# Gated cross-attention with a routed expert layer on one core: routing work reordered across engines in the first pairs of tiles, the loops over slots written out, the passage between the stages rearranged, and a small matmul put ahead of the scores

## The chip, the cores and the metric

The kernel runs on one core of one Trainium2 chip. The metric is the device time of one execution in microseconds (us). Of the kernel before, three runs gave 657.65, 660.46 and 661.85 us, so its median is 660.46 us. One more execution was profiled; it took 661.32 us, of which 659.5 us lie between its first and its last instruction.

## The reference, cut to what matters

```python
# x, ctx: (16, 256, 256); wq, wk, wv: (256, 256); Wg: (8, 256); W1, W2: (8, 704, 256); W3: (8, 256, 704)
def attention(q, c, wq, wk, wv):          # queries from c, keys and values from q
    Q, K, V = c @ wq, q @ wk, q @ wv
    return softmax(Q @ K.T, axis=2) @ V

def experts(x, Wg, W1, W2, W3):           # 4096 tokens
    scores = x @ Wg.T
    topk_scores, topk_idx = top_k(scores, 2)
    y = einsum('teh,edh->ted', silu(x @ W1) * (x @ W2), W3)
    return sum over the two chosen experts of topk_scores * y

x = x + tanh(g_xattn[0]) * attention(ctx, layernorm(x), wq, wk, wv)
x = x + tanh(g_ffn[0]) * experts(layernorm(x), Wg, W1, W2, W3)
```

## The kernel before

The work has two stages on the same five engines. Engine programs are written out by hand, one per engine, and are tied together by semaphores; nothing reorders them. An engine that waits holds up everything behind it in its own program.

**First stage, steps n = 0 to 15, one batch of 256 rows each.** TensorE multiplies the context with the weights (`z`, `v`), forms the scores, sums, turns the probabilities and multiplies them with the values. ScalarE copies results out of PSUM, takes the exponents, and squares the weights of half an expert per step (`squares`, lines 682 to 693). `weight_sum` (line 865) adds these squares over the partitions on TensorE, VectorE makes the power of two out of them by which that half expert is scaled (`scales`, line 1041), and ScalarE (`w_hi`, line 715) and VectorE (`lo12`, `lo3`, lines 1061 to 1074) split the scaled weights into two float16 parts. VectorE also adds the residual, takes the second moments of the new rows and routes ten of the sixteen batches already here: `AT_STEP` (line 71) says at which step batch m is routed. To route a batch takes a chain over four engines: `second_moments` (VectorE), the power -1/2 (GpSimd, `deviations` or `second_deviations`), `high_rows` (VectorE) and `norm_rows` (ScalarE) for the two parts of the normed rows, `low_rows` (GpSimd), `turn_rows` and `router` (TensorE, ScalarE copying between them by `copy_rows`), `choose` (VectorE, the two best experts), `rank` (TensorE, the place within the expert), `slots` (VectorE) and `scatter` (GpSimd, four indirect DMAs that write the rows into a buffer in HBM sorted by expert).

**Second stage, slots i = 0 to 38.** Slots 0 to 31 are pairs of tiles of 128 rows of one expert, 32 to 38 single tiles. SP fetches the rows of slot i+2, TensorE turns them (`turn_gathered`), ScalarE copies them, TensorE multiplies with W1 (`to_hidden`, 36 matmuls), ScalarE applies silu (`gate`), TensorE multiplies with W2 (30 matmuls), VectorE multiplies the two (`mixed` for the piece of 64 partitions, `combined` for the rest), ScalarE and VectorE split the result (`high`, `low`), TensorE multiplies with W3 (`to_output`, 17 matmuls for each tile), ScalarE scales it (`copy_product`) and GpSimd adds it to the rows in HBM (`add_rows`, an indirect DMA that adds). Each such add waits until the one before it has landed. The last six batches are routed during the pairs 0 to 5 (`AT_PAIR`, line 72), so that batch 10+i goes through the chain above in pair i. When all are placed, VectorE works out the list of slots 8 to 38 (`other_slots`, lines 1251 to 1283) and releases it by `s_map`; before that SP cannot fetch slot 8.

`over_slots` (line 401) lets each engine run its step for slots -2 to 7 written out, 8 to 23 as two passes of a loop with eight steps in it, and the rest written out again. GpSimd has a loop of its own for the slots 8 to 31 (line 633).

The rows of rsqrt in the pairs are made by these lines, in this order (lines 626 to 632 of GpSimd's program):

```python
for i in range(EARLY):
    if i + 1 in AT_PAIR:
        second_deviations(AT_PAIR[i + 1])
        low_rows(AT_PAIR[i + 1])
    if i in AT_PAIR:
        scatter(AT_PAIR[i])
    add_rows(i, i % 4)
```

Of the kernel before, what the change touches and what calls it, by code (L numbers as in the profile page):

```python
# [7 lines left out]
ALU = mybir.AluOpType  # L8
# [8 lines left out]
P = 128  # L17
# [6 lines left out]
def gated_cross_attention_and_experts(nc, x, ctxT, g_xattn, g_ffn, wqT, wkT, wv, WgT, W1T, W2T, W3T, out):  # L24
# [70 lines left out]
    with ExitStack() as ctx:  # L95
# [253 lines left out]
        def pair(i):  # L349

            return not isinstance(i, int) or i < PAIRS
# [13 lines left out]
        def at_least(eng, s, v):  # L365

            if not (isinstance(v, int) and v <= 0):
                eng.wait_ge(s, v)

        def wait_alone(eng, s, v):  # L370


            if not isinstance(v, int):
                v = eng.to_reg(v)
                eng.wait_ge(s_const, CONSTS)
                eng.wait_ge(s, v)
            elif v > 0:
                eng.wait_ge(s, v)
# [22 lines left out]
        def over_slots(eng, step, take=lambda i, n: None, planned=lambda: None):  # L401


            def written(a, b):
                for i in range(a, b):
                    step(i, i // 2, i % 4, i % UNROLL, lambda m: 0 <= m < SLOTS)
# [16 lines left out]
        def _(sp):  # L423
# [59 lines left out]
            for k in range(2):  # L483
                sp.wait_ge(s_scat[k], 16 * KT * TOP_K * ((COUNTED + 1 - k) // 2))
                sp.wait_ge(s_x2st[k], 16 * (5 - k))
            sp.wait_ge(s_xn2, 9)
# [18 lines left out]
            def moe_step(i, j, k4, u, on):  # L505
                k = k4 % 2
                if isinstance(i, int) and i == EARLY - 2:
                    pads()
                    all_rows()
                if on(i + 2):  # L510

                    wait_alone(sp, s_id, i + 1)
# [8 lines left out]
        def _(pool):  # L521
# [85 lines left out]
            scatter(IN_STEPS - 1)  # L607
            low_rows(IN_STEPS)
# [5 lines left out]
            def add_rows(i, k4):  # L614

                for t, half, t8 in tiles(i, k4):
                    if t8 % 2 == 0:
                        if not (isinstance(t, int) and t == 0):
                            pool.wait_ge(s_add[1], 16 * half)
                    else:  # L620
                        pool.wait_ge(s_add[0], 16 * half + 16)
                    wait_alone(pool, s_y_copied, t + 1)
                    pool.indirect_dma_start(  # L623
                        out=out[:, :], out_offset=bass.IndirectOffsetOnAxis(ap=id_s[:, t8:t8 + 1], axis=0),
                        in_=y_s[:, t8 % 4, :], in_offset=None, compute_op=ALU.add).then_inc(s_add[t8 % 2], 16)
# [12 lines left out]

        @block.scalar
        def _(act):  # L640
# [40 lines left out]

            def squares(u):
# [10 lines left out]
                ins.then_inc(s_sq, 1)  # L693

# [740 lines left out]
```

## Time and profile before

| what | us |
|---|---|
| median of three runs | 660.46 |
| lowest, highest | 657.65, 661.85 |
| the profiled execution | 661.32 |
| its span, first to last instruction | 659.5 |
| TensorE busy with matmuls | 589.5 (89%) |
| VectorE, ScalarE, GpSimd busy | 318.4, 329.6, 269.1 |
| mean granted clock of TensorE | 0.962 of full speed |

In the page and the answers PE is TensorE, PEld its weight loads, DVE VectorE, ACT ScalarE, POOL GpSimd and SPq, ACTq, POOLq the DMA queues. A granted clock of 1.00 is TensorE's 2.4 GHz, 0.50 would be 1.2 GHz. Matmuls overlap in the records, so the time of a group is best taken from its start to the start of the next. A bracket behind a row says how long the engine was idle before it, and who ended that. Idle time of an engine costs time only where that engine's work is what the end waits for; here TensorE has most of it, so the gaps in its row are what is to be explained.

### The profile page before, as it was taken

How to read it: one execution, taken by the hardware profiler on the slowest of the kernel's cores; microseconds unless marked ns; L12 is line 12 of the kernel's file. 1: busy time of each engine (PE TensorE's matmuls, PEld its weight loads, DVE VectorE, ACT ScalarE, POOL GpSimd, SP SyncE). 2: the span in 40 equal slices, each digit the busy share in tenths (PEclk: the TensorE clock that was granted, in tenths of full speed). 3: DMA queues.
4: the chain of work that ended last, by engine and by line, in shares of the span. 5: the costliest groups of instructions: out<-in, count | busy, mean ns of one | idle time of the engine just before them, and what ended most of it. 6: DMA issues, size and time to landing. Idle time of an engine off the chain costs nothing.

```text
span 659.5 us, 15092 instructions
## 1 busy us (share of the span) xinstructions
PE 589.5 (89%) x4765; PEld 511.8 (78%) x4766; DVE 318.4 (48%) x860; ACT 329.6 (50%) x474; POOL 269.1 (41%) x245
## 2 busy tenths in 40 slices
PE   5898989898688967789699999799999999999995
PEld 4787878777567855678598989698989898988783
DVE  2488877797656434456333333243433343343332
ACT  3778787887734243433344444244444444444442
POOL 3155565655513655546133333223233333333322
PEclk9899999999878987899799999899999999999999
DMA  8476666855412322215232323132323232322322
GB/s 254 142 233 188 219 203 220 258 169 165 149 35 85 68 60 68 59 34 138 58 59 43 58 36 52 31 54 43 59 43 59 42 56 39 52 42 43 50 43 25
DMA packets 52372, 61.53 MB, mean 93 GB/s; under 512 B 7632, under 2 KB 46160, under 8 KB 52304
## 3 DMA queue, kind: packets, MB, share of 16 engines
q1 hardware_dynamic: 34656, 38.15, 19.2%
q0 software_dynamic: 13296, 18.23, 16.0%
q10 hardware_dynamic: 4352, 4.20, 1.8%
q8 instruction: 48, 0.79, 0.5%
q14 instruction: 20, 0.16, 0.1%
HBM read 36.90 MB, written 23.66 MB: 92 GB/s over the span
## 4 chain that ended last, share of the span: by engine, by line
PE 61%; DVE 12%; ACT 10%; issue 8%; POOL 5%; DMA 2%; another core or an unknown queue 1%; SPq 0%; POOLq 0%; ACTq 0%; DVEq 0%
PE psum L923 30%; PE psum L963 18%; PE psum L818 4%; PE psum L932 4%; PE psum L943 2%; DMA w_in<-in_W3T 2%; ACT w_hi L715 2%; POOL rows_by_expert L586 2%; DVE w_lo L1072 2%; ACT arena L678 2%; ACT w_hi L687 1%; ACT w_hi L691 1%; DVE w_lo L1065 1%; POOL out L623 1%; PE psum L856 1%
## 5 line engine op out<-in xcount | busy, mean ns | idle before, releaser
L623 POOL DMA_INDIRECT out<-w_in,id_s x71 | 126.8, 1786 | 249.2 <-ACT w_in L767 132.4
L923 PE MATMUL psum<-arena,w_hi 128*128 128x256 f16 x1408 | 217.3, 278 | 5.5 <-issue 4.1
L923 PEld LDWEIGHTS psum<-arena,w_hi 128*128 x1408 | 140.3, 100 | 24.7 <-issue 6.2
L923 PE MATMUL psum<-arena,w_lo 128*128 128x256 f16 x704 | 136.9, 277 | 0.0
L749 ACT ACTIVATE arena<-psum 128x1024 f16<-128x1024 f16 (+1 forms) x39 | 36.9, 947 | 95.3 <-PE psum L943 94.8
L818 PE MATMUL psum<-arena 128*128 128x256 f32 x256 | 66.3, 404 | 19.0 <-ACT arena L701 19.0
L1353 DVE SCALAR_TENSOR_TENSOR arena<-psum,h_unit,arena 128x1280 f32<-128x1280 f32 x32 | 49.6, 1550 | 63.8 <-PE psum L923 63.8
L586 POOL DMA_INDIRECT rows_by_expert<-xn2r,slot_i x64 | 66.3, 1036 | 33.8 <-issue 17.4
L923 PEld LDWEIGHTS psum<-arena,w_lo 128*128 x704 | 70.2, 100 | 9.3
L818 PEld LDWEIGHTS psum<-arena 128*128 128x128 f32 x256 | 47.9, 197 | 28.0 <-ACT arena L701 22.4
L1347 DVE SCALAR_TENSOR_TENSOR arena<-psum,h_unit,arena 64x256 f32<-64x256 f32 x32 | 15.7, 491 | 92.3 <-ACT arena L740 92.2
L738 ACT ACTIVATE arena<-psum,w_unscale 64x256 f32<-64x256 f32 x32 | 15.0, 468 | 89.4 <-PE psum L923 89.3
L963 PE MATMUL psum<-w_hi,arena 128*128 x396 | 57.7, 281 | 2.2 <-DVE arena L1370 2.2
L963 PE MATMUL psum<-w_hi,w_in 128*128 x385 | 55.5, 280 | 0.0
L767 ACT ACTIVATE w_in<-psum,wsum 128x256 f32<-128x256 f32 x71 | 33.2, 467 | 43.8 <-PE psum L963 21.9
L963 PEld LDWEIGHTS psum<-w_hi,arena 128*128 128x128 f16 x396 | 38.9, 101 | 7.7 <-issue 2.4
L740 ACT ACTIVATE arena<-psum,w_unscale 128x1280 f32<-128x1280 f32 x32 | 42.5, 1328 | 0.4
L963 PEld LDWEIGHTS psum<-w_hi,w_in 128*128 128x128 f16 x385 | 37.6, 100 | 5.1
L715 ACT ACTIVATE w_hi<-w_in,w_scale 128x1408 f16<-128x1408 f32 x16 | 23.5, 1468 | 24.6 <-DVE w_scale L1047 18.2
L963 PE MATMUL psum<-w_lo,arena 128*128 x216 | 31.5, 284 | 0.0
L818 PE MATMUL psum<-arena,qk 128*128 128x256 f32 x128 | 30.6, 382 | 0.0
L943 PE MATMUL psum<-ident,xa 128*128 128x128 f16 x284 | 22.6, 221 | 8.7 <-DMA xa<-rows_by_expert 5.9
(183 smaller groups left out, 906.4 us busy)
## 6 DMA issues: line engine op xcount, KB each, us to landing
xa<-rows_by_expert SPq DMA_DIRECT2D x71, 136.0 KB
w_in<-in_W1T SPq DMA_DIRECT2D x8, 704.0 KB
w_in<-in_W3T SPq DMA_DIRECT2D x8, 640.0 KB
w_in<-in_W2T SPq DMA_DIRECT2D x8, 640.0 KB
arena<-in_ctxT SPq DMA_DIRECT2D x16, 256.0 KB
xa<-in_x SPq DMA_DIRECT2D x16, 256.0 KB, 6.0
out<-xa ACTq DMA_DIRECT2D x16, 256.0 KB
out<-w_in,id_s POOLq DMA_INDIRECT x71, 4.4
```

The source lines that it names most:

```text
L586: pool.indirect_dma_start(out=xs[:, :], out_offset=bass.IndirectOffsetOnAxis(ap=slot_i[:, k, col:col + 1], axis=0), in_=xn2r[:, m % ROWS, ...
L623: pool.indirect_dma_start(out=out[:, :], out_offset=bass.IndirectOffsetOnAxis(ap=id_s[:, t8:t8 + 1], axis=0), in_=y_s[:, t8 % 4, :], in_of ...
L715: act.activation(w12[0][:, :, n * H:(n + 1) * H], w12_in[:, k], ACT.Copy, scale=w_scale[:, 0:1].bitcast(F32)).then_inc(s_hi12, 1)
L740: act.activation(act_g[:, 0:KF * N2], g_ps, ACT.Silu, scale=w_unscale[:, 0, bass.ds(expert[u], 1)].bitcast(F32)).then_inc(s_silu, 1)
L749: act.activation(xg_t[:, k, :, :, 0:n], xt_ps[:, :, :, 0:n], ACT.Copy).then_inc(s_xgt, 1)
L767: act.activation(y_s[:, t8 % 4, :], y_ps[t8 % 2], ACT.Copy, scale=wsum[:, t8:t8 + 1]).then_inc(s_y_copied, 1)
L818: ins = pe.matmul(dst[:, t, :], left[:, c, t * P:(t + 1) * P], right[:, c, :], start=(c == 0), stop=(c == 1))
L923: ins = pe.matmul(flat_ps[:, j * N2:(j + 1) * N2], w12[w_part][:, c, bass.ds(e * (2 * H) + j * P, P)], xg_t[:, k, x_part, c, :], start=(q ...
L932: ins = pe.matmul(dst, xg_t[:, k, x_part, c, 0:P], w12[w_part][:, c, bass.ds(e * (2 * H) + at, n)], start=(q == 0 and c == 0), stop=(q == ...
L943: ins = pe.transpose(xt_ps[:, h, c, half * P:(half + 1) * P], xg[:, k, half, at:at + P // 2].bitcast(F16), ident16[:])
L963: ins = pe.matmul(y_ps[t8 % 2], hid_p[k4 % 2][:, c * n + h * P:c * n + (h + 1) * P], w3[w_part][:, r, bass.ds(e * D, D)], start=(q == 0), ...
L1353: dve.scalar_tensor_tensor(out=hid[:, 0:KF * N2], in0=u_ps, scalar=h_unit[:, 0, bass.ds(e, 1)].bitcast(F32), in1=act_g[:, 0:KF * N2], op0= ...
```

## The change

It computes the same. On each engine it changes where work stands in the program:

- **The sum of squares in front of the scores.** `weight_sum(n)` moves on TensorE from behind `router` and `rank` to ahead of the scores of step n. It gets waits of its own: for `s_rcopy` (that `choose` of the batch routed in step n-1 is through) and for `s_place`, because its result lies in the PSUM bank of the router. `router` and what follows wait for `s_half` of the same step. On VectorE `scales` moves ahead of `slots`.
- **The passage.** Slot 0 is turned and copied within step 15 (ahead of `values(14)` and of ScalarE's `w_hi` of step 15). SP fetches slot 0 a wait earlier. TensorE begins slot 0 when `s_lo12` is 15, and waits for 16 only before the sixth chunk; `turn_probs(15)` moves behind the first four chunks. ScalarE's last `w_hi` of W3, the table of silu and the wait for `s_unit` go behind step 15. `units` moves forward on VectorE, `choose(9)` ahead of `lo3(7)`.
- **The pairs with routing.** GpSimd works out the power of batch 10+i+1 in pair i, behind `low_rows` of batch 10+i, and the two adds of a pair are set apart, one at each end of its turn. GpSimd's wait for the stores of all batches (`s_x2st`) now stands ahead of `scatter(9)` and `low_rows(10)`. VectorE has `high_rows` at the front of the step and `second_moments` ahead of `combined`; ScalarE has `norm_rows` ahead of the copies; TensorE has `rank` behind the second half of the output of slot i-2.
- **Slots written out.** The loops go; all 39 slots are written out on every engine.

The core of the diff:

```diff
 # over_slots
-            written(-2, 0)
-            take(0, EARLY)
-            written(0, EARLY)
-            planned()
-            with eng.Fori(0, 2) as r:
-                take(UNROLL * r + EARLY, UNROLL)
-                for u in range(UNROLL):
-                    step(UNROLL * r + EARLY + u, UNROLL // 2 * r + (EARLY + u) // 2, u % 4, u, lambda m: True)
-            take(PAIRS - UNROLL, UNROLL)
-            written(PAIRS - UNROLL, PAIRS)
-            take(PAIRS, SINGLES)
-            written(PAIRS, SLOTS + 1)
+            for i in range(-2, SLOTS + 1):
+                if i >= 0 and i % UNROLL == 0:
+                    if i == EARLY:
+                        eng.wait_ge(s_map, 2)
+                    take(i, min(UNROLL, SLOTS - i))
+                step(i, i // 2, i % 4, i % UNROLL, lambda m: 0 <= m < SLOTS)
 # GpSimd
             second_deviations(IN_STEPS)
-            scatter(IN_STEPS - 1)
-            low_rows(IN_STEPS)
 
             for k in range(2):
                 pool.wait_ge(s_x2st[k], 16 * (B // 2))
             pool.wait_ge(s_dummy, 16)
...
-            for i in range(EARLY):
-                if i + 1 in AT_PAIR:
+            for i in range(SLOTS + 1):
+                if i >= 2 and pair(i - 2):
+                    add_rows(i - 2, 1)
+                if i == 0:
+                    scatter(IN_STEPS - 1)
+                if i - 1 in AT_PAIR:
+                    scatter(AT_PAIR[i - 1])
+                if i in AT_PAIR:
+                    low_rows(AT_PAIR[i])
+                if i + 1 in AT_PAIR and i >= 0:
                     second_deviations(AT_PAIR[i + 1])
-                    low_rows(AT_PAIR[i + 1])
-                if i in AT_PAIR:
-                    scatter(AT_PAIR[i])
-                add_rows(i, i % 4)
-            with pool.Fori(EARLY // 4, PAIRS // 4) as q:
-                for k4 in range(4):
-                    add_rows(4 * q + k4, k4)
-            for i in range(PAIRS, SLOTS):
-                add_rows(i, i % 4)
+                if i >= 1:
+                    add_rows(i - 1, 0)
 # TensorE, first stage
             def weight_sum(u):
 
                 pe.wait_ge(s_sq, u + 1)
                 at_least(pe, s_half, u)
+                if u - 1 in AT_STEP:
+                    pe.wait_ge(s_rcopy, AT_STEP[u - 1] + 1)
+                if u - 2 in AT_STEP:
+                    pe.wait_ge(s_place, AT_STEP[u - 2] + 1)
...
                 if live(n):
+                    weight_sum(n)
                     pe.wait_ge(s_z_copied, n + 1)
                     pe.wait_ge(s_t1_copied, n + 1)
                     product(sc_ps, x_t, z_s).then_inc(s_sc, 1)
                 if n in AT_STEP:
                     router(AT_STEP[n])
+                if live(n):
+                    pe.wait_ge(s_half, n + 1)
+                if n - 1 in AT_STEP:
+                    rank(AT_STEP[n - 1])
                 if n == COUNT_STEP:
                     count(COUNTED)
-                if n - 1 in AT_STEP:
-                    rank(AT_STEP[n - 1])
-                if live(n):
-                    weight_sum(n)
+                if n == B - 1:
+                    pe.wait_ge(s_t1_copied, B)
+                    turn_gathered(0, 0, 0)
                 if live(n - 1):
                     values(n - 1)
...
-            pe.wait_ge(s_lo12, 2 * E)
             pe.wait_ge(s_map, 1)
 # VectorE, pairs
                 if chosen:
                     choose(AT_PAIR[at - 1])
+                if at in AT_PAIR:
+                    high_rows(AT_PAIR[at])
                 if on(i):
                     if pair(i):
                         mixed(i, expert[u])
                     weights_and_rows(i, j, k4, expert[u])
                     if at == 0:
                         residual(B - 1)
+                        slots(IN_STEPS - 1)
...
-                    if at in AT_PAIR:
-                        high_rows(AT_PAIR[at])
+                    if at + 1 in AT_PAIR:
+                        second_moments(AT_PAIR[at + 1])
                     combined(i, expert[u])
-                    if at == 0:
-                        slots(IN_STEPS - 1)
                     low(i, k)
```

GpSimd's program in one of the pairs with routing, from the first add of a pair on. In the kernel before both adds stand together, the power of the next batch comes behind them, and the rows of that batch directly behind the power:

```order
L623 DMA out<-w_in,id_s 4224x256 [waits s_y_copied,s_add1]
L623 DMA out<-w_in,id_s 4224x256 [waits s_y_copied,s_add0]
L574 TENSOR_SCALAR var_eps<-mv 128x2 [waits s_rcopy,s_mv2]
L576 TENSOR_TENSOR rstd<-var_eps,neg_half 128x2 [waits s_ve]
L595 COPY xn2r<-token 128x2 [waits s_xh,s_xf]
L596 TENSOR_TENSOR xn2r<-arena,xn2r 128x2x256
L586 DMA rows_by_expert<-xn2r,slot_i 33792x272 [waits s_xn2,s_slot]
L586 DMA rows_by_expert<-xn2r,slot_i 33792x272 x3
```

In the changed kernel, at the same place:

```order
L603 DMA out<-w_in,id_s 4224x256 [waits s_y_copied,s_add1]
L603 DMA out<-w_in,id_s 4224x256 [waits s_y_copied,s_add0]
L569 DMA rows_by_expert<-xn2r,slot_i 33792x272 [waits s_xn2,s_slot]
L569 DMA rows_by_expert<-xn2r,slot_i 33792x272 x3
L578 COPY xn2r<-token 128x2 [waits s_xh,s_xf]
L579 TENSOR_TENSOR xn2r<-arena,xn2r 128x2x256
L557 TENSOR_SCALAR var_eps<-mv 128x2 [waits s_rcopy,s_mv2]
L559 TENSOR_TENSOR rstd<-var_eps,neg_half 128x2 [waits s_ve]
```

The power (L574, L576; now L557, L559) moved behind `low_rows`, and belongs to the batch after the one whose rows are made there; the first add is that of the pair before. The program is a cycle, so that the two adds still stand side by side.

TensorE's program in a step of the first stage in which one batch goes through the router and the one before it is ranked, before:

```order
L818 MATMUL psum<-arena 128x256 [waits s_t1_copied,s_z_copied]
L818 MATMUL psum<-arena 128x256 x3
L856 MATMUL psum<-wg_c,arena 128x8 [waits s_half,s_place,s_wg,s_rcopy,s_t2_copied]
L856 MATMUL psum<-wg_c,arena 128x8 x3
L831 MATMUL psum<-mask,before 128x16 [waits s_seen1,s_rcopy]
L832 MATMUL psum<-seen,ones 128x16
L870 MATMUL psum<-ssq,ones_f 128x1 [waits s_half,s_sq]
```

and in the changed kernel:

```order
L872 MATMUL psum<-ssq,ones_f 128x1 [waits s_rcopy,s_half,s_sq]
L803 MATMUL psum<-arena 128x256 [waits s_t1_copied,s_z_copied]
L803 MATMUL psum<-arena 128x256 x3
L841 MATMUL psum<-wg_c,arena 128x8 [waits s_half,s_place,s_wg,s_rcopy,s_t2_copied]
L841 MATMUL psum<-wg_c,arena 128x8 x3
L816 MATMUL psum<-mask,before 128x16 [waits s_seen1,s_rcopy,s_half]
L817 MATMUL psum<-seen,ones 128x16
```

The sum of squares moved to the front and now waits for `s_rcopy`; the scores are queued behind it.

## Rows read from the trace of the kernel before

**Rows 1.** The page, its first line.

```profile
span 659.5 us, 15092 instructions
```

**Rows 2.** Busy time of engines by stretch; a row: stretch, length, engines, PEclk, DMA, GB/s.

```profile
17.40:184.47 167.07, 143.31 (x783) 123.56 (x781) 127.34 (x433) 133.62 (x228) 90.99 (x97) 0.97 0.60 192
184.47:198.73 14.26, 13.19 (x97) 10.86 (x98) 6.39 (x26) 4.58 (x6) 0.41 (x1) 0.84 0.08 24
198.73:286.93 88.20, 70.74 (x595) 59.79 (x595) 39.05 (x139) 31.11 (x43) 46.50 (x48) 0.88 0.27 66
286.93:322.53 35.60, 26.77 (x222) 22.29 (x221) 21.79 (x65) 12.63 (x15) 17.49 (x14) 0.86 0.37 95
322.53:413.60 91.07, 91.07 (x866) 81.76 (x863) 33.40 (x47) 40.03 (x48) 29.81 (x16) 1.00 0.29 49
413.60:424.00 10.40, 6.30 (x43) 5.02 (x44) 1.91 (x2) 1.66 (x3) 2.26 (x1) 0.84 0.13 18
```

**Rows 3.** Waits between 18 and 180 us: waited for, us, times, longest.

```profile
PE psum L818 <- ACT arena L701: 19.0, 14, 2.8
ACT w_hi L715 <- DVE w_scale L1047: 18.2, 11, 3.2
```

**Rows 4.** Timeline of PE, scores of step 12: start, us, what, [idle before].

```profile
138.84 1.99 PE L818 MATMUL psum<-arena 128*128 128x256 f32 x8 [1.17 <-ACT arena L701]
```

**Rows 5.** Timeline of DVE, steps 11 and 12.

```profile
132.10 1.65 DVE L1134 TENSOR_TENSOR nbias<-nmax,rstd 128x2 f32<-128x2 f32 x1
...
140.23 0.35 DVE L1183 SCALAR_TENSOR_TENSOR xn2r<-psum,rstd,mask 128x8 f32<-128x8 f32 x2
...
143.71 0.44 DVE L1134 TENSOR_TENSOR nbias<-nmax,rstd 128x2 f32<-128x2 f32 x1
```

**Rows 6.** Timeline of PE, the passage from step 15 to slot 0.

```profile
171.58 3.42 PE L818 MATMUL psum<-arena 128*128 128x256 f32 x8 [2.76 <-ACT arena L701]
...
180.92 0.61 PE L943 MATMUL psum<-ident,xa 128*128 128x128 f16 x8 [2.77 <-DVE w_lo L1065]
...
184.47 1.03 PE L923 MATMUL psum<-arena,w_hi 128*128 128x256 f16 x4 [1.40 <-ACT arena L749]
```

**Rows 7.** Timeline of POOL, one pair with routing.

```profile
260.34 1.61 POOL L623 DMA_INDIRECT out<-w_in,id_s  x1 [0.30 <-issue]
264.45 1.59 POOL L623 DMA_INDIRECT out<-w_in,id_s  x1 [2.50 <-DMA out<-w_in,id_s]
...
266.39 0.73 POOL L576 TENSOR_TENSOR rstd<-var_eps,neg_half 128x2 f32<-128x2 f32 x1
271.98 0.96 POOL L595 COPY xn2r<-token 128x2 int32<-128x2 int32 x1 [4.87 <-ACT arena L659]
...
274.22 1.07 POOL L586 DMA_INDIRECT rows_by_expert<-xn2r,slot_i  x1 [0.17 <-issue]
...
279.42 1.62 POOL L623 DMA_INDIRECT out<-w_in,id_s  x1 [0.30 <-issue]
```

**Rows 8.** Waits of the whole execution.

```profile
DVE shift L1104 <- POOL rstd L576: 35.7, 4, 9.4
...
PE psum L831 <- DVE xn2r L1183: 19.8, 6, 5.4
```

**Rows 9.** Timeline of PE, pairs 4 to 8 and 16.

```profile
263.61 0.60 PE L811 MATMUL psum<-ident,xa 128*128 128x128 f32 x4
...
266.35 0.96 PE L856 MATMUL psum<-wg_c,arena 128*128 128x8 f32 x8
...
293.93 0.18 PE L831 MATMUL psum<-mask,before 128*128 128x16 bf16 x1 [2.90 <-DVE xn2r L1183]
...
318.42 1.01 PE L943 MATMUL psum<-ident,xa 128*128 128x128 f16 x8 [5.93 <-DMA xa<-rows_by_expert]
...
417.70 1.02 PE L923 MATMUL psum<-arena,w_hi 128*128 128x256 f16 x4 [4.10 <-issue]
```

**Rows 10.** Timeline of DVE, first instruction of the list of slots.

```profile
306.14 0.15 DVE L1253 SCALAR_TENSOR_TENSOR begin<-done,region_of 1x8 f32<-1x8 f32 x1
```

More of the change, by code:

```diff
@@ L349, in pair @@
         def pair(i):
-            return not isinstance(i, int) or i < PAIRS
+            return i < PAIRS
         def tiles(i, k4):
@@ L365, in at_least @@
         def at_least(eng, s, v):
[L367 to L377, printed above, removed]
+            if v > 0:
                 eng.wait_ge(s, v)
@@ L506, in moe_step @@
                 k = k4 % 2
-                if isinstance(i, int) and i == EARLY - 2:
+                if i == -1:
+                    sp.wait_ge(s_xn2, 9)
+                    sp.wait_ge(s_x2st[0], 16 * 5)
+                if i == EARLY - 2:
                     pads()
@@ L763, in copy_product @@
                 act.wait_ge(s_wsum, i + 1)
-                if not (isinstance(t, int) and t < 4):
+                if t >= 4:
                     act.wait_ge(s_add[t8 % 2], 16 * (half - 1))
@@ L778, in moe_step @@
                 if at in AT_PAIR:
+                    norm_rows(AT_PAIR[at])
                     copy_rows(AT_PAIR[at], x10_ps)
-                if on(i + 1):
+                if i >= 0 and on(i + 1):
                     copy_turned(i + 1, 1 - k)
@@ L863, in count, with turn_gathered @@
                 pe.matmul(cnt_ps, ones[:], seen[:, m % 2, 0, :], start=True, stop=True).then_inc(s_cnt, 1)
+            def turn_gathered(i, j, k):
+                pe.wait_ge(s_row[k], landed(i, j))
+                for half in range(2 if pair(i) else 1):
+                    for h in range(2):
+                        for c in range(KD):
+                            at = h * (D // 2) + c * (P // 2)
+                            ins = pe.transpose(xt_ps[:, h, c, half * P:(half + 1) * P],
+                                               xg[:, k, half, at:at + P // 2].bitcast(F16), ident16[:])
+                ins.then_inc(s_xt, 1)
             def weight_sum(u):
@@ L934, in to_hidden_rows @@
                 return ins
-            def turn_gathered(i, j, k):
-                pe.wait_ge(s_row[k], landed(i, j))
-                for half in range(2 if pair(i) else 1):
-                    for h in range(2):
-                        for c in range(KD):
-                            at = h * (D // 2) + c * (P // 2)
-                            ins = pe.transpose(xt_ps[:, h, c, half * P:(half + 1) * P],
-                                               xg[:, k, half, at:at + P // 2].bitcast(F16), ident16[:])
-                ins.then_inc(s_xt, 1)
             def turn_hidden(i):
@@ L999, in moe_step @@
                         to_hidden_rows(g1_ps[:, 1, :], HB - HL, HB, expert[u], k).then_inc(s_g, 1)
-                    if at is not None and at - 1 in AT_PAIR:
-                        rank(AT_PAIR[at - 1])
-                        if AT_PAIR[at - 1] == B - 1:
-                            count(B)
                 if on(i - 2) and pair(i - 2):
                     to_output(i - 2, (k4 - 2) % 4, 1, expert[u - 2])
+                if at == 0:
+                    rank(IN_STEPS - 1)
+                if at - 1 in AT_PAIR and at > 0:
+                    rank(AT_PAIR[at - 1])
+                    if AT_PAIR[at - 1] == B - 1:
+                        count(B)
                 if on(i):
@@ L1332, in weights_and_rows @@
                 dve.wait_ge(s_row[k], landed(i, j))
-                if not (isinstance(i, int) and i < 4):
+                if i >= 4:
                     dve.wait_ge(s_y_copied, ts[-1][0] - 7)
@@ L1336, in weights_and_rows @@
                                   ALU.mult).then_inc(s_wsum, 1)
-                if not (isinstance(i, int) and i < 4):
+                if i >= 4:
                     for t, half, t8 in ts:
```

100 lines of the change are left out of this document (49 added, 51 removed).

## The prediction

> **What bounds the kernel now.** I read the busy time by stretch first [rows 2]. The steady pairs show what the kernel can do: pairs 8 to 15 take 91.07 us, all of it TensorE's at full clock, so a pair is 11.4 us and nothing but fewer matmuls shortens it. The stretches to be won are those where TensorE has gaps. The first stage lasts 167 us, 24 of them without a matmul. Slot 0 takes 14.3 us. The five pairs 1 to 5 take 88.2 us, pairs 6 and 7 35.6 us, and around pair 16 there is a hole. I call S the start of the scores of step 15 (171.58 [rows 6]), G1 the start of pair 1 (198.73), G6 that of pair 6 (286.93), G8 that of pair 8 (322.53) [rows 2].
>
> Then I read the waits. In the first stage TensorE waits 19.0 us for the copy of z, and ScalarE 18.2 us for the scale of the weights [rows 3]. In the pairs VectorE's `high_rows` waits up to 9.4 us for GpSimd's power, and TensorE's `rank` 19.8 us over six times for `choose` [rows 8]. GpSimd's timeline says why [rows 7]: first add at 260.34, the second 4.1 us later because it waits for the first to land, then the power, then 4.87 us without work until ScalarE has made the normed rows that wait for this very power (`high_rows`, `combined`, `high` and `norm_rows` stand between), then four scatters, and the next first add at 279.42. That ring is 19.1 us long, and pairs 2 to 5 run at its pace, not at TensorE's.
>
> **The change part by part.** The sum is made against the profiled execution: a span of 659.5 us [rows 1] and 1.8 us around it, 661.3, which is 0.9 over the median.
>
> *Pairs 1 to 5.* A pair with routing needs 11.4 us of TensorE and two small groups, at most 0.60 + 0.96 us by their rows, some 1.3 as they overlap with what follows [rows 2, 9]: 12.7 us. With the power a pair ahead the ring is cut: `high_rows` finds its power made, and ScalarE makes the rows while GpSimd scatters. What stays is GpSimd's own work in a row: 4.1 from the first add to the second, 1.9 for that one, 5.2 for the scatters, 2.2 for copy and `low_rows`, 1.0 for the power, together 14.4 us [rows 7]; where the copy takes 0.2 instead of 0.96, 13.6. This is 1 to 1.7 us a pair more than TensorE needs. The lag gathers over four pairs to 4 to 7 us. I take it that most of it is absorbed: a power needed for `high_rows` may come late by about 2 us before `combined` is late, and `combined` and `choose` have about 2.5 more before TensorE needs them. I charge 1 us.
>
> Pair 1 has a wait of its own. GpSimd may now scatter batch 9 only when the stores of batches 14 and 15 have landed, and ScalarE issues these behind `high(0)`, about 2 us after G1. With 3.5 us to land (an estimate; the trace shows no row for it; bounds 2 and 6), 4.9 for the scatters, 1.3 and 1.0, the power of batch 11 comes at G1 + 13, and behind it `high_rows`, `mixed` and `slots` at G1 + 15, which the router of batch 11 waits for. So pair 1 takes 15.9 instead of 12.7. The gap of 3 us on TensorE is followed by slow matmuls, as everywhere here: pairs 1 to 5 run at a mean clock of 0.88 [rows 2]. I charge 1.6. Sum: 5 x 12.7 + 3.2 + 1.6 + 1.0 = 69.3 against 88.2, a gain of 18.9 (bounds: 25 with no wait at all; 13 if GpSimd sets all five pairs at 14.4 and the stores land late).
>
> *The passage, S to G1.* Today 27.2 us. TensorE waits 2.77 us for `lo12` before it turns slot 0 and 1.40 for ScalarE, which does the last W3 and loads the silu table first [rows 6]. Both go, since slot 0 is turned and copied within step 15. The first chunks run at half clock now, 1.03 us for four matmuls [rows 6] against 0.60 later; the stretch from 184.47 has a mean clock of 0.84, which is 2.3 us of work lost [rows 2]. The scores at S are slow as well, 3.42 us against 1.99 [rows 4, 6]. I count 4.2 of waits, 2.3 and 1.4 of clock: 7.9. What is late next is `values(15)`, because ScalarE does W3 and the table (about 3 us) ahead of the copy of the probabilities; six chunks of slot 0 cover that. Bounds 3 (a new wait there, the clock stays low) and 10.
>
> *Pairs 6 and 7.* The wait of 2.90 us for `rank` [rows 9] goes as low work of pair 5 is earlier, with 1.6 of slow clock behind it. The list of slots stays: it starts at 306.14 [rows 10], and 12.3 us later TensorE turns slot 8 [rows 9]. It hangs on `low(6)`, which stays in its place, so TensorE's wait of 5.9 stays too. Gain 4.5 (bounds 2 and 6).
>
> *The loops.* At the start of pair 16, where the second pass begins, TensorE waits 4.10 us for nothing that the trace shows [rows 9]. It is the only pair boundary in the stage with such a wait, and the only one at which a taken branch lies. The stretch of 10.40 us holds 6.30 of matmuls, at 0.84 [rows 2]: 4.1 and 1.8 of clock, 5.9 us gained. Bounds: 0, if filling the instructions of a written-out pair costs as much once, and 6.
> The Trainium skill, "Runtime: NRT & Kernel Launch", section "Instruction fetch mechanics", says that prefetch is purely sequential and that a taken branch to a target outside the window stops the engine for a fetch. The trace agrees, with the 4.10 us.
>
> *The first stage.* ScalarE's 18.2 us of waiting for the scale go, but the exponents behind `w_hi` need the scores and VectorE's maxima, which don't come sooner in a step where a batch is ranked. There the change costs: the scores are queued behind `weight_sum`, which now waits for `choose`. In step 12 `choose` writes its last piece at 140.23 + 0.35, the scores started at 138.84 [rows 4, 5]: 1.9 us later. There are nine such steps among 3 to 15. In the other steps the maxima come 0.3 us earlier and `w_hi` 1 us, and the step shortens by 1 to 1.8 us. Adding up a cycle of three steps on TensorE, VectorE and ScalarE I get 30.8 where the trace has 31.3. Steps 0 and 1, with nothing routed, give 2. In all 3.5 us gained (bounds 8 gained, 5 lost).
> One row speaks of a clash: VectorE's `nbias` takes 1.65 us at 132.10 and 0.44 at 143.71 [rows 5]; the first lies over GpSimd's `low_rows`. It is there before as after, so I count nothing.
> The Trainium skill, "SBUF — State Buffer", section "Who interferes with whom", says that a VectorE instruction with two SBUF inputs contends with a GpSimd instruction that reads SBUF, and that the second fully blocks. The 1.65 us agree. By it the sum would lose up to 1.5 us wherever the moved `scales` and maxima fall on `low_rows` anew, 7.5 for five steps; by the row, none.
>
> Sum: 18.9 + 7.9 + 4.5 + 5.9 + 3.5 = 40.7; 661.3 - 40.7 = 620.6, against the median 660.46 some 619.7.
>
> **The rivals.**
> 1. *The scores behind `choose` lengthen the first stage.* For it: 1.9 us in nine steps [rows 4, 5], and VectorE, busy 127 of 167 us [rows 2], can't simply be earlier. Against it: in the step after, ScalarE gains back what it waited [rows 3]. If nothing is gained back: 9 x 1.9 = 17 lost instead of 3.5 gained, 640.
> 2. *The pairs stay at GpSimd's old pace.* If another wait takes the place of the power (the landing of an add, the stores), pairs 1 to 5 stay near 88: 619.7 + 18.9 = 639. Against it: GpSimd's work in a row is 14.4, and its idle 4.87 is caused by the power alone [rows 7].
> 3. *Slower: written-out slots stall TensorE on its instructions.* The 16 pairs of the loop are now fetched as straight code. Each stall like that at pair 16 costs 5.9 [rows 2, 9]; six of them eat the other gains (34.8), and from eight on the kernel is slower by over 1%; one in each of 16 would give 625.6 + 94 = 720. Against it: pairs 0 to 7 and 24 to 31 are straight code today and show no such gap.
> 4. *1 and 2 together*, about 659: no change that can be told.
>
> **How the numbers follow.** Chances: forecast 0.76, with a range of its own from 608 to 633 (the bounds of the parts, which are 13 to 25, 3 to 10, 2 to 6, 0 to 6 and -5 to 8, added as independent deviations give about -11 and +13); rival 1 0.10; rival 2 0.07; both 0.03; rival 3 0.02; 0.02 for more gain than the range. The range takes in rivals 1 and 2: 608 to 640. One per cent (6.6 us) is about what a measurement of this kernel can tell from no change. Faster by over 1%: 0.76 + 0.10 + 0.07 + 0.02 = 0.95; same 0.03; slower 0.02.
>
> **What would show it.** Pairs 2 to 5: starts of `to_hidden` 12.7 to 14.4 us apart; GpSimd without the 4.9 us gap before its copy; no wait of `high_rows` over 3 us but in pair 1. Pair 1: near 16 us, ended by `slots`. Passage: S to G1 near 19 us. Slot 8: still a wait of about 6 us for the rows. Pair 16: no gap. First stage: scores start right behind `choose` in ranked steps, and S lies at 168. I am wrong if S is later than 172, if pairs 2 to 5 are over 16 us apart, or if gaps "issue" turn up in pairs 8 to 23.

## The result and the profile after

The changed kernel takes 626.7 us (median of 4 runs, 626.39 to 627.07) against 660.87 us (657.65 to 661.85) before, measured side by side: a ratio of 0.950, 95% interval 0.947 to 0.953. The profiled execution has a span of 625.0 us, 34.5 less than before [rows 1]. By the marks of the prediction:

| stretch | before, us | after, us | gained | forecast |
|---|---|---|---|---|
| start to S | 171.58 | 173.64 | -2.1 | 3.5 |
| S to G1 | 27.15 | 18.45 | 8.7 | 7.9 |
| G1 to G6 | 88.20 | 69.42 | 18.8 | 18.9 |
| G6 to G8 | 35.60 | 31.66 | 3.9 | 4.5 |
| G8 to the end | 336.97 | 331.83 | 5.1 | 5.9 |

The busy time by stretch, columns as in [rows 2], which it answers:

```profile
17.40:173.64 156.24, 140.13 (x747) 121.46 (x745) 115.04 (x407) 125.55 (x215) 88.98 (x89) 0.96 0.63 198
173.64:192.09 18.45, 16.86 (x136) 14.52 (x136) 14.90 (x54) 13.43 (x21) 6.32 (x8) 1.00 0.24 76
192.09:208.06 15.97, 11.83 (x105) 10.26 (x106) 6.63 (x28) 5.50 (x7) 7.04 (x9) 0.97 0.21 70
208.06:261.51 53.45, 53.45 (x489) 47.56 (x490) 33.90 (x109) 26.62 (x37) 36.96 (x40) 0.95 0.36 84
261.51:293.17 31.66, 24.38 (x222) 21.23 (x222) 20.94 (x62) 10.86 (x13) 18.62 (x15) 0.89 0.46 115
384.24:570.00 185.76, 185.76 (x1762) 166.71 (x1761) 70.16 (x100) 83.41 (x100) 61.99 (x33) 1.00 0.28 47
```

Pairs 2 to 5 (208.06 to 261.51) are now TensorE's without a gap, 12.66 us each in three of the four. The written-out slots at 384.24 to 570.00 have no gap either: the hole of [rows 9] at pair 16 is gone. What is left is a gap in pair 1, one in pair 7, and a first stage that became longer. The gain of 18.8 us from G1 to G6 isn't spread evenly: before, pairs 1 to 5 took 15.05, 13.98, 19.66, 19.74 and 19.77 us (starts of `to_hidden`), now they take 15.97, 15.47 and three times 12.66. So pairs 3 to 5 give 21.2 us, and pairs 1 and 2 are 2.4 us slower.

The waits of the first stage on TensorE (waited for, us, times, longest; to be read beside the 19.0 us of [rows 3], which are gone):

```profile
PE psum L872 <- DVE xn2r L1179: 9.4, 6, 2.3
PE psum L841 <- DVE halves L1041: 4.4, 2, 3.0
PE psum L872 <- ACT w_hi L676: 1.2, 1, 1.2
```

L872 is `weight_sum` (the sum of squares), L1179 the last piece of `choose`, L841 the router, L1041 the shift that makes the scale (`scales`, which signals `s_half`). The second row is a wait that the prediction doesn't have: the router of a step waits for that step's scale, since both are in PSUM bank 7. The timeline of TensorE in step 14 shows what it drags along:

```profile
157.69 1.99 PE L803 MATMUL psum<-arena 128*128 128x256 f32 x8
162.71 1.84 PE L841 MATMUL psum<-wg_c,arena 128*128 128x8 f32 x8 [3.03 <-DVE halves L1041]
164.41 3.76 PE L803 MATMUL psum<-arena 128*128 128x256 f32 x8
...
173.64 1.97 PE L803 MATMUL psum<-arena 128*128 128x256 f32 x8
```

After a gap of 3.03 us the values take 3.76 us, where the scores at S, with no such gap ahead, take 1.97. The stretch behind this gap, and the first 5.4 us of pair 2, behind the gap that ends pair 1, have a granted clock of 0.50, which is the level of 1.2 GHz (busy time by stretch, columns as above):

```profile
162.71:168.00 5.29, 5.29 (x17) 4.46 (x18) 0.77 (x3) 2.61 (x6) 4.29 (x6) 0.50 0.87 314
208.06:213.50 5.44, 5.44 (x27) 3.88 (x28) 3.81 (x10) 1.85 (x2) 4.52 (x6) 0.50 0.47 153
```

This one step is where the first stage loses. The scores of step 14 start at 157.69, against 159.22 before; from there to S it takes 15.95 us, against 12.36. In step 14 VectorE makes the scale only behind `high_rows`, and `high_rows` waits for GpSimd's power (timeline of VectorE):

```profile
161.58 0.16 DVE L1100 SCALAR_TENSOR_TENSOR shift<-mv,rstd 128x2 f32<-128x2 f32 x1 [0.95 <-POOL rstd L550]
162.32 0.14 DVE L1041 TENSOR_SCALAR halves<-psum 128x1 int32<-128x1 int32 x1
```

The busy time of the first stage up to S in the kernel before, to be read beside the first row of the busy time after:

```profile
17.40:171.58 154.18, 135.16 (x742) 117.15 (x740) 120.25 (x410) 124.46 (x214) 84.25 (x89) 0.99 0.62 199
```

TensorE is without a matmul for 16.1 us now and was for 19.0 us before. Its gaps became shorter, by 2.9 us; what makes S later are 5.0 us more of matmul time, at a mean clock of 0.96 instead of 0.99. The 5.29 us at half clock in step 14 are 2.6 of these 5.0.

Pair 1, on GpSimd, VectorE and TensorE (timelines):

```profile
197.29 1.03 POOL L569 DMA_INDIRECT rows_by_expert<-xn2r,slot_i  x1 [13.09 <-DMA out<-xa]
...
204.55 0.16 DVE L1100 SCALAR_TENSOR_TENSOR shift<-mv,rstd 128x2 f32<-128x2 f32 x1 [7.73 <-POOL rstd L559]
...
206.67 1.54 PE L841 MATMUL psum<-wg_c,arena 128*128 128x8 f32 x8 [3.58 <-DVE place L1112]
```

The scatters of batch 9 start when the stores have landed, G1 + 5.2 (forecast 5.5). That the two numbers are close is luck: ScalarE issues the last stores at 191.90 to 192.80, at G1 and not 2 us behind it, and they land 4.5 to 5.4 us later, not 3.5. `high_rows` starts at G1 + 12.5, the router of batch 11 at G1 + 14.6 (forecast 13 and 15). GpSimd in the pairs after, which answers [rows 7]:

```profile
240.36 1.17 POOL L579 TENSOR_TENSOR xn2r<-arena,xn2r 128x512 f16<-128x512 f32 x1
241.61 0.19 POOL L557 TENSOR_SCALAR var_eps<-mv 128x2 f32<-128x2 f32 x1
241.89 0.73 POOL L559 TENSOR_TENSOR rstd<-var_eps,neg_half 128x2 f32<-128x2 f32 x1
243.24 1.75 POOL L603 DMA_INDIRECT out<-w_in,id_s  x1 [0.62 <-ACT w_in L751]
247.52 1.56 POOL L603 DMA_INDIRECT out<-w_in,id_s  x1 [2.53 <-DMA out<-w_in,id_s]
249.39 1.00 POOL L569 DMA_INDIRECT rows_by_expert<-xn2r,slot_i  x1 [0.30 <-issue]
```

The idle 4.87 us ahead of its copy is gone; the next first add is at 256.95, a ring of 13.7 us instead of 19.1.

### The profile page after: what moved, and what is told of

The parts are those of the page before. It is cut to its first block, busy times and chain, and to the rows that moved or that the text cites. A ratio compares the mean times of both kernels' runs of the same rounds, so it can differ in the third digit from the quotient of the medians.

```text
span 625.0 us, 14783 instructions
## 1 busy us (share of the span) xinstructions
PE 581.5 (93%) x4765; PEld 510.1 (82%) x4765; DVE 315.8 (51%) x859; ACT 329.6 (53%) x473; POOL 271.7 (43%) x245
## 4 chain that ended last, share of the span: by engine, by line
PE 78%; DVE 10%; ACT 4%; issue 3%; POOL 2%; DMA 1%; POOLq 0%; SPq 0%; DVEq 0%; ACTq 0%
PE psum L928 34%; PE psum L957 20%; PE psum L803 12%; PE psum L937 4%; PE psum L857 2%; PE psum L841 2%; PE psum L796 2%; DVE w_lo L1068 1%; DVE w_lo L1061 1%; PE psum L946 1%; ACT w_hi L664 1%; DVE xa L1139 1%; DMA out<-xa 1%; DVE stats L1147 1%; ACT arena L659 1%
## 5 line engine op out<-in xcount | busy, mean ns | idle before, releaser
L928 PE MATMUL psum<-arena,w_hi 128*128 128x256 f16 x1408 | 213.4, 275 | 0.5 <-DVE xa L1139 0.4
L928 PEld LDWEIGHTS psum<-arena,w_hi 128*128 x1408 | 138.0, 99 | 17.8 <-issue 1.0
L928 PE MATMUL psum<-arena,w_lo 128*128 128x256 f16 x704 | 135.4, 274 | 0.0
L569 POOL DMA_INDIRECT rows_by_expert<-xn2r,slot_i x64 | 68.4, 1069 | 34.0 <-issue 17.7
L957 PE MATMUL psum<-w_hi,w_in 128*128 x385 | 53.5, 273 | 0.0
L751 ACT ACTIVATE w_in<-psum,wsum 128x256 f32<-128x256 f32 x71 | 33.2, 467 | 18.8 <-PE psum L957 18.8
L803 PE MATMUL psum<-wv_s,arena 128*128 128x256 f32 x128 | 30.2, 379 | 0.0
```

The lines of the kernel that those rows point to most:

```text
L569: pool.indirect_dma_start(out=xs[:, :], out_offset=bass.IndirectOffsetOnAxis(ap=slot_i[:, k, col:col + 1], axis=0), in_=xn2r[:, m % ROWS, ...
L751: act.activation(y_s[:, t8 % 4, :], y_ps[t8 % 2], ACT.Copy, scale=wsum[:, t8:t8 + 1]).then_inc(s_y_copied, 1)
L803: ins = pe.matmul(dst[:, t, :], left[:, c, t * P:(t + 1) * P], right[:, c, :], start=(c == 0), stop=(c == 1))
L928: ins = pe.matmul(flat_ps[:, j * N2:(j + 1) * N2], w12[w_part][:, c, bass.ds(e * (2 * H) + j * P, P)], xg_t[:, k, x_part, c, :], start=(q ...
L957: ins = pe.matmul(y_ps[t8 % 2], hid_p[k4 % 2][:, c * n + h * P:c * n + (h + 1) * P], w3[w_part][:, r, bass.ds(e * D, D)], start=(q == 0), ...
```

## The experiments

Marks of all kernels, us, each from one profiled execution; the ratio is to the kernel before on the same chip, with its 95% interval:

| kernel | S | S to G1 | G1 to G6 | G6 to G8 | from G8 | ratio |
|---|---|---|---|---|---|---|
| before | 171.58 | 27.15 | 88.20 | 35.60 | 336.97 | 1 |
| after | 173.64 | 18.45 | 69.42 | 31.66 | 331.83 | 0.950 (0.947, 0.953) |
| 1 sum put back | 170.63 | 20.25 | 68.94 | 33.64 | 331.34 | 0.949 (0.945, 0.953) |
| 2 sum alone | 173.86 | 23.45 | 87.85 | 35.77 | 336.37 | 1.000 (0.998, 1.002) |
| 3 own bank | 166.02 | 20.19 | 67.18 | 33.30 | 331.91 | 0.936 (0.933, 0.939) |
| 4 own bank, scale wait kept | 173.59 | 18.46 | 69.67 | 34.04 | 331.34 | 0.949 (0.944, 0.954) |
| 5 own bank, `choose` wait kept | 170.96 | 19.98 | 68.61 | 33.15 | 332.10 | 0.953 (0.948, 0.958) |
| 6 stores later | 174.61 | 18.67 | 62.68 | 33.41 | 331.93 | 0.947 (0.943, 0.952) |
| 7 power back | 171.88 | 18.46 | 79.39 | 33.25 | 331.42 | 0.966 (0.963, 0.970) |
| 8 scatter back | 173.86 | 18.47 | 70.16 | 33.54 | 331.27 | 0.958 (0.953, 0.963) |
| 9 turn later | 177.67 | 18.49 | 67.08 | 33.19 | 332.07 | 0.950 (0.945, 0.955) |
| 10 unrolled alone | 170.61 | 27.47 | 88.45 | 35.49 | 331.78 | 0.994 (0.992, 0.996) |
| 11 bank and stores | 163.65 | 21.37 | 62.69 | 33.88 | 331.01 | 0.930 (0.927, 0.934) |
| 12 list early | 161.34 | 20.09 | 62.79 | 28.46 | 331.82 | 0.923 (0.918, 0.928) |

S spreads by some us between kernels whose code is the same up to there: 173.6, 174.6, 171.9, 173.9 and 177.7 in after, 6, 7, 8 and 9, and 166.0, 163.7, 161.3 in 3, 11 and 12. So S is compared by groups. S to G1 repeats within 0.3 us but for kernel 11 (21.37, where its group has 20.1 and 20.2), G6 to G8 within 0.9 but for the profile of after (31.66, where all kernels with its code there have 33.2 to 34.0). From the scores of step 14 to S it takes 15.9 to 16.0 us in after, 2, 6, 7, 8 and 9, 15.6 in kernel 4, and 11.4 to 12.7 in before, 1, 3, 5, 10, 11 and 12: it is long exactly where the router waits for the scale of its own step.

**1. The sum put back.** On TensorE:

```
+ product(sc_ps, x_t, z_s); router(m); count; rank(m - 1); weight_sum(n)
- weight_sum(n); product(sc_ps, x_t, z_s); router(m); wait(s_half, n + 1); rank(m - 1); count
```

and `scales` behind `slots` on VectorE, with the old waits.

> The changed kernel with the sum of squares of the weights alone put back behind the ranking on TensorE, and the scale back behind the slots on VectorE. S, the start of the scores of step 15, was 171.58 before the change and 173.64 after it. Theory (the sum in front of the scores costs the first stage its time, because it waits for `choose` and makes the router wait for the scale): S near 171.6, the two waits of TensorE (9.4 us for `choose` ahead of `weight_sum`, 4.4 us of `router` for `scales`) gone, time 624.6. Rival (the loss comes from somewhere else, the passage or the order of step 15): S stays at 173.6 and the time at 626.7. By the prediction's own term (3.5 gained by this part) the run would be slower: S 175, 630.

The time is the same, 626.4 us, though S is 3.0 us earlier: 1.8 of it is lost again between S and G1. The theory had the stage right and the price wrong: 624.6 was expected. The step to S takes 11.44 us instead of 15.95, so the sum in front costs 4.5 us in this one step; in the steps ahead of it kernel 1 is 1.5 us behind.

**2. The sum alone**, the reverse edit in the kernel before.

> The kernel before with the sum of squares in front of the scores as the only edit. Theory: the first stage loses about 2 us, S near 173.6; behind S nothing is touched, so 660.9 + 2 = 663. Rival (the prediction's term): S near 168, 657.4. Second rival (the passage gains only because the scale comes earlier in step 15): S to G1, the start of pair 1, falls from 27.2 us by more than 1 us.

S comes at 173.86, 2.3 us later, as the theory said, but S to G1 gets 3.7 shorter, as the second rival said. The rest of the passage follows VectorE and ScalarE, which are not late by what TensorE loses. In sum the time doesn't change. S in three profiles with the sum behind (before, 1, 10) is 170.6 to 171.6, in the six with it in front and with nothing else done to it (after, 2, 6 to 9) 171.9 to 177.7.

**3. Own bank.**

```
- ssq_ps = bank[7][:, 192:194]
+ ssq_ps = bank[1][:, 0:2]
- weight_sum: wait(s_rcopy), wait(s_place), wait(s_plan)
- router: wait(s_half, STEP_OF[m] + 1);  rank: wait(s_half, n + 1)
+ ahead of z: wait(s_half, n);  weight_sum behind wait(s_z_copied, n + 1)
+ ahead of slot 0: wait(s_half, B)
```

> The changed kernel with the sum of squares written into the bank of z (two columns, once z is copied) instead of the bank that the router, the ranks and the count share. Then `weight_sum` need not wait for `choose`, nor `router` and `rank` for the scale; z of the next step waits for the scale instead. Theory (the waits for the shared bank eat what the early scale gives): the 9.4 and 4.4 us of TensorE's waits go, the exponents get the scale early, S at 165 to 169, time 618 to 622. Rival (VectorE's own queue sets the step, the waits of TensorE only stand where it would wait anyway): S at 171 to 174, 624 to 627.

S is 166.02 and the time 618.4 us; the interval lies wholly under that of the changed kernel. TensorE's waits up to step 15:

```profile
PE psum L864 <- ACT arena L691: 11.8, 10, 2.1
```

Neither `choose` nor the scale is in the list; what is left is the copy of z. The gain in the first stage was to be had, and the shared bank had kept it.

**4 and 5. Which of the two waits.** Own bank, with one of the waits put back: that of `router` and `rank` for the scale (4), or that of `weight_sum` for `choose` (5).

> The kernel with the sum of squares in the bank of z (618.4 us, S at 166.02), but `router` and `rank` of each step wait for the scale of that step again, as in the changed kernel. It tells the two waits of the changed kernel apart: that of `weight_sum`, and so of the scores, for `choose` (9.4 us in six waits), and that of the router for the scale (4.4 us in two). If the first is the one that costs: S stays near 166 to 167, 618.4 to 619.5. If it is the second: S goes back to 171 or later, 623 to 627. If both share it, S near 169, 622.

> The kernel with the sum of squares in the bank of z (618.4 us, G1 at 186.21), but `weight_sum`, and so the scores behind it, waits for `choose` again. The counterpart of the run in which the router kept its wait for the scale (625.9 us, G1 at 192.05). If the router's wait is the whole cost: G1 near 186, time 618 to 619.5. If the prediction's 1.9 us in nine steps cost as much when they stand alone: G1 at 190 or later, 623 to 627.

The first has 625.9 us and G1 at 192.05, the second 628.3 us and G1 at 190.94; own bank has G1 at 186.21. TensorE's waits in the first stage, kernel 4, then kernel 5:

```profile
PE psum L839 <- DVE halves L1036: 8.2, 6, 2.6
PE psum L864 <- ACT arena L691: 3.9, 5, 1.7
```

```profile
PE psum L870 <- DVE xn2r L1177: 11.0, 5, 2.5
PE psum L870 <- ACT arena L691: 6.0, 3, 3.1
```

In kernel 4 the copy of z is waited for less by 7.9 us than in kernel 3, and the scale 8.2 us instead. Either wait alone costs the gain (all of it in the times; to G1 5.8 us in kernel 4 and 4.7 in kernel 5, of 5.9), and both together cost no more than one. So the prices don't add: I had expected the one or the other, or a share of each.

The two cost it in different ways. TensorE's gaps between 17.40 us and S are 12.3 us in kernel 3, 13.0 in kernel 4 and 17.8 in kernel 5; the mean clock is 0.99, 0.95 and 0.99. The wait for `choose` costs gaps. The wait for the scale costs 0.7 us of gaps and 6.8 us more of matmul time, in slow matmuls such as the values of step 14, 3.76 us again behind a gap of 2.61.

**6. The stores later.** GpSimd's `wait(s_x2st)` and `wait(s_dummy)` moved from the front of its pairs to just ahead of the first `add_rows`.

> The changed kernel in which GpSimd waits for the stores of batches 14 and 15 only ahead of the first added rows, not ahead of the scatters of batch 9. Theory (pair 1 is long because GpSimd waits until 197.29 for the stores, then scatters, and `rank`, `choose` and the router wait for the power behind that): pair 1 falls from 15.97 to about 12.7 us, its half-clock matmuls go too, time 622 to 623.5. Rival (the time goes to the next link: GpSimd's own ring of 13.7 to 14.1 us a pair takes it back in pairs 2 to 5): pair 1 short, pairs 2 to 5 longer in sum by the same, G1 to G6 still near 69, 626.

Pair 1 falls from 15.97 to 11.96 us and pair 2 from 15.47 to 12.74 (in the changed kernel the clock is 0.50 in its first 5.4 us, here it is 1.00 throughout). G1 to G6 is 6.7 us shorter; 1.8 comes back in pairs 6 and 7 beside the profile of after, which is the odd one there, and this profile's S is 1.0 later. The median, 624.4 us, alone wouldn't tell it from the changed kernel; the trace does, and so does kernel 11.

**7 and 8. What cut the ring.** In 7 GpSimd's power stands behind the adds of its own pair again, ahead of the scatters; in 8 the power is ahead, but the scatters stand behind `low_rows` again.

> The changed kernel with GpSimd's power alone moved back: it is no longer made a pair ahead behind `low_rows`, but behind the two adds of its own pair, ahead of the scatters. The scatters stay between the power and `low_rows`. Theory of the prediction (the power a pair ahead cuts the ring): pairs 2 to 5 go back to 16 to 19 us, G1 to G6 78 to 85 us, time 636 to 643. Rival (the scatters between power and `low_rows` hide VectorE's and ScalarE's work by themselves, GpSimd's own work in a row is the same 14 us): G1 to G6 at most 73 us, time 627 to 630.

> The changed kernel with GpSimd's scatters alone moved back behind `low_rows` and the power; the power is still a pair ahead. It is the counterpart of the run with the power moved back (G1 to G6 79.4 us, 635.9). Theory (both moves are needed: the scatters between give ScalarE time for the rows): GpSimd waits for the rows ahead of `low_rows` again, by up to 3 us, G1 to G6 73 to 80 us, 630 to 637. Rival (the power ahead is the whole gain): G1 to G6 within 1.5 us of 69.4, 626 to 628.

With the power back pairs 2 to 5 take 15.5 to 17.7 us and G1 to G6 10.0 more. GpSimd in kernel 7:

```profile
231.44 1.56 POOL L603 DMA_INDIRECT out<-w_in,id_s  x1 [3.06 <-DMA out<-w_in,id_s]
233.07 0.19 POOL L557 TENSOR_SCALAR var_eps<-mv 128x2 f32<-128x2 f32 x1
233.35 0.73 POOL L559 TENSOR_TENSOR rstd<-var_eps,neg_half 128x2 f32<-128x2 f32 x1
236.71 1.06 POOL L569 DMA_INDIRECT rows_by_expert<-xn2r,slot_i  x1 [2.63 <-DVE slot_i L1121]
```

The power holds up `high_rows`, this `slots`, and `slots` the scatters: 2.63 us of idling that the ring pays in each pair. With the scatters back G1 to G6 is only 0.7 longer. So the power a pair ahead carries 10.0 of the 18.8 us, and the place of the scatters by itself next to nothing. The other 8.8 stay in kernel 7, where pairs 3 to 5 take 16.5 us on average against 19.7 before; they belong to the moves that it keeps (`high_rows` in front, the two adds set apart, `norm_rows` ahead of the copies, `rank` later), which no run took apart. The median of 8 is 4.5 us over that of the changed kernel, of which its trace, the quickest of its runs, shows 2.3; where the rest lies I can't say.

**9. Turn later.** Slot 0 turned and copied behind step 15, as before.

> The changed kernel with one part of the passage put back: TensorE turns slot 0 behind the values of batch 14 and ScalarE copies it behind the exponents of step 15, not within step 15. Theory (slot 0 turned and copied in time is what took TensorE's waits of 2.77 and 1.40 us and the slow matmuls behind them away): S to G1 grows from 18.45 to 21.5 to 22.5, G1 near 195.5, time 629.5 to 630.5. Rival (W3 and the silu table behind the copy are what counts, the turn is late enough anyway): S to G1 at most 20, time under 628.5.

My theory fell. S to G1 is 18.49 us, the 18.45 of the changed kernel; the time is 627.3. TensorE has a gap of 1.58 us ahead of slot 0 (at 184.34) in place of waits of 0.91 and 0.40 us that the changed kernel has within slot 0. Turning slot 0 within step 15 is worth nothing. What gives the passage its 8.7 us is the sum in front (3.7 by kernel 2, 1.8 by kernel 1) and the other moves together: W3 and the silu table behind the copy, the later wait for `lo12`. These others were not taken apart.

**10. Unrolled alone** in the kernel before.

> The kernel before with the slots 8 to 31 written out on every engine as the only edit, no loop. Theory (the taken branch at pair 16 costs 4.10 us of gap and 1.8 us of slow clock): the gap is gone, the part behind G8 falls from 337.0 to about 331, time 655. Rival (the straight code pays the same fetch elsewhere): the part behind G8 stays at 337, 660.7. What stands before G8 should not move in either.

The part from G8 on is 5.2 us shorter, nothing moves ahead of it, and the time falls by 4.0 us. TensorE's busy time around what was the gap:

```profile
322.02:413.00 90.98, 90.98 (x867) 81.91 (x865) 33.33 (x47) 39.83 (x48) 29.82 (x16) 1.00 0.30 49
413.00:430.00 17.00, 17.00 (x162) 15.28 (x161) 6.16 (x8) 7.92 (x10) 6.07 (x3) 1.00 0.24 39
```

**11 and 12. A better kernel.** 11 is 3 and 6 together; in 12 GpSimd also scatters batch 15 between its two adds, and VectorE writes the list ahead of `low(6)`:

```
+ if i == EARLY - 2: scatter(B - 1)
  add_rows(i - 2, 1)
...
+ if chosen and AT_PAIR[at - 1] == B - 1: other_slots()
  low(i, k)
```

> Both repairs at once: the sum of squares in the bank of z, and GpSimd's wait for the stores only ahead of the first added rows. Theory (both gains are real until G6, and what ends pairs 6 and 7 is GpSimd's last scatters and the list of slots): G1 near 186, G1 to G6 near 63, pairs 6 and 7 33 to 35 us, time 614 to 616. Rival (GpSimd, whose own ring is 13.7 to 14.1 us a pair, sets slot 8 and gives the second gain back): 617 to 618.5, no better than the bank alone.

> On top of both repairs (612.4 us, TensorE's wait for the rows of slot 8 8.8 us): GpSimd scatters batch 15 between the two adds of a pair, where it waits for the first add to land, and VectorE writes the list of the slots ahead of `low(6)` and not behind it. Theory (slot 8 waits for the later of the last scatter's landing and the list; TensorE doesn't need `low(6)` before slot 8 is turned): the list ends 3 to 4 us sooner, the wait falls from 8.8 to 4.5 to 6, pairs 6 and 7 take about 30 us, time 608 to 610. Rival (the wait goes over to `low(6)` or the second add): pairs 6 and 7 stay at 33 to 34, 612.

Kernel 11 has 612.4 us, with pairs 2 to 5 at 12.66 us each, and TensorE waits 8.8 us for the rows of slot 8. In kernel 12 that wait is:

```profile
268.80 1.01 PE L857 MATMUL psum<-ident,xa 128*128 128x128 f16 x8 [2.73 <-DMA xa<-rows_by_expert]
```

Its time is 608.3 us, a ratio of 0.923 (0.918 to 0.928): it beats both kernels, by 8% and by 3%. So the wait at slot 8 hangs on the list and the last scatters together, and moves with them; which of the two counts was not tried.

## Why the prediction was right, and where not

The forecast was 619.7 us, 7.0 below what came; the time lies in the range, and also in the likeliest case's own (608 to 633).

*The first stage* is the term that was mis-sized, by 5.6 us: "In all 3.5 us gained (bounds 8 gained, 5 lost)", and 2.1 were lost. "I am wrong if S is later than 172" came true. The prediction saw one of the two new waits, the 1.9 us behind `choose`, and then added up a cycle in which the earlier scale more than paid for it. For the gaps it was nearly right: TensorE's became 2.9 us shorter. It left out the other wait, and the clock: the router now waits for the scale, 3.03 us in step 14, and the 5.3 us behind run at 0.50. That step alone is 3.6 us longer than before. Kernels 4 and 5 show that each of the two waits holds the stage back by itself, kernel 3 that without them some 8 us come back. That is not rival 1 at its price (17 us lost), but its mechanism in part. The marks also show a flaw of the sum: S is a mark on TensorE, and what is lost ahead of it comes back behind it in part. Counted to G1 the sum in front costs 1.2 us (after against 1) or gives 1.4 (2 against before), which is nothing beside the spread of S.

*The passage* gave 8.7 against 7.9, for reasons that were partly wrong. The waits of 2.77 and 1.40 us did go [rows 6], and the clock at S and in slot 0 is full now (1.97 us for the scores, 0.60 for four matmuls). But "both go, since slot 0 is turned and copied within step 15" is refuted by kernel 9: they go without it, and the 1.58 us that come there cost nothing.

*Pairs 1 to 5* came out as the sum had them: 18.8 against 18.9, pair 1 15.97 against 15.9, by the chain that was named (stores, scatters, power, `slots`, router). One reading was wrong: "pairs 2 to 5 run at its pace" holds for pairs 3 to 5 (19.7 us each); pair 2 took 13.98 before, and the total that the gain is reckoned from hides it. The 3.5 us for the stores to land had no row, and no run shows this figure: landing took 4.5 to 5.4 us, from a start 2 us earlier. The charge for GpSimd's lag was 1.0; pairs 3 to 5 show none. That for the clock, 1.6, was low: kernel 6 wins 6.7 us from pair 1's wait, where the sum had 4.8. Kernel 7 confirms the power as a cause, against rival 2, but for 10.0 us and not for all 18.8.

*Pairs 6 and 7*: 4.5 forecast, 3.9 in this profile, about 2 in the nine others with the changed code there (33.2 to 34.0). The wait for slot 8 stayed, as said, and even grew (5.93 us [rows 9], 7.28 in this profile, 6.5 to 8.8 in the others). What TensorE gains ahead of it by the missing wait for `rank` is handed to it in part.

*The loops*: 5.1 against 5.9. Kernel 10 isolates them, 5.2 in the trace and 4.0 in the medians; so behind the gap of 4.10 the clock cost about 1.1, not 1.8. Rival 3, written-out slots that stall, isn't there: 185.76 us without a gap.
The Trainium skill ("Runtime: NRT & Kernel Launch", section "Instruction fetch mechanics") says that a taken branch to a page outside the current window has to wait for a fetch of it. Kernel 10 agrees: with the branch the 4.10 us go.

*The range.* Added as independent deviations, the bounds give -8 and +13, not -11 and +13. The time lies inside either way.

## What to carry to other kernels

Before moving an instruction ahead of another, list who else writes or reads its PSUM bank: the waits that keep the order there move with it, and may lie on the very step that was to be sped up; a bank that is free at that time was worth 8 us here. Don't judge a stage by the sum of its gaps: here the gaps shrank by 2.9 us and the stage grew by 2.1, because slow matmuls followed the longest of them. Take the starts of all pairs, not their mean, before saying what pace they run at. Price a ring between two engines by what each does in a row after the move, and ask which instruction of the next round can be made a round ahead. Gains ahead of a chain that ends on another engine (here the list and the scatters before slot 8) are given back until that chain is moved as well.

## What the runs showed of the hardware

Two waits on one step cost as much as either alone: G1 at 192.05 with one, 190.94 with the other, 192.09 with both and 186.21 with none.

Where the gaps lie counts beside how long they are in sum. Before, TensorE had 14 waits of 0.77 to 2.8 us in the first stage at a mean clock of 0.99. Now the waits are fewer and one is 3.03 us; behind it the clock is 0.50, the level of 1.2 GHz, for 5.3 us, and the mean is 0.96.

The Trainium skill ("PSUM — Partial Sum Buffer", section "PSUM bank collisions raise a hardware error") says that two engines must not be in one bank on the same partitions at once, in whichever columns; that is why the four small tiles of bank 7 wait for each other. No run here took such a wait away within a bank, so the rule is not tested.

VectorE and GpSimd hold each other up where I had counted nothing. In kernel 6 VectorE multiplies two inputs in SBUF (1x880) while GpSimd scatters:

```profile
276.35 1.06 DVE L1271 TENSOR_TENSOR w_in<-w_in,gap 1x880 f32<-1x880 f32 x1
```

```profile
276.40 1.86 POOL L569 DMA_INDIRECT rows_by_expert<-xn2r,slot_i  x1 [0.30 <-issue]
278.57 0.97 POOL L569 DMA_INDIRECT rows_by_expert<-xn2r,slot_i  x1 [0.30 <-issue]
```

The scatter at 276.40 takes 1.86 us instead of 0.97, longer by about what the multiplication still had to run. It recurs: in kernels 1 and 11 the scatter that starts 0.04 and 0.05 us behind the same instruction takes 1.86 us as well, and in the changed kernel one takes 2.04 us over the multiplication of `low` (1.49 us from 262.67, the scatter at 262.99). In kernel 8, where no scatter lies over the 1x880 multiplications, they take 0.96 to 1.23. That VectorE's instruction blocks GpSimd's fits all of these; no run was made to vary it alone.
The Trainium skill ("SBUF — State Buffer", section "Who interferes with whom") says that a VectorE instruction with two SBUF inputs contends with a GpSimd instruction that reads SBUF, over ports that only one of them can hold at a time; these rows agree, by 0.9 to 1.1 us each. The 7.5 us that the prediction gave for that rule in the first stage didn't come: kernels 3 to 5 find the loss in the bank, and `nbias`, the prediction's own example, takes 3.4 us in its sixteen steps after and 6.5 before. The 0.44 us that the prediction took as its undisturbed time lies over `low_rows` too; in eleven of the sixteen steps before it is 0.16.
